# Mixer front: time-step projection and softplus one chunk earlier, the running sum and its exponentials in the third chunk, and the exponential table turned back after each part

## What is computed

```python
zxbcdt = u @ W_in.T
z0 = zxbcdt[..., :D_INNER]
x0 = zxbcdt[..., D_INNER:2 * D_INNER]
xBC = zxbcdt[..., 3 * D_INNER:3 * D_INNER + D_XBC]
dt = jax.nn.softplus(zxbcdt[..., -NHEADS:] + dt_bias)
A = -jnp.exp(A_log)
xBC = silu(causal_depthwise_conv(xBC, conv_w) + conv_b)      # 4 taps
x, Bm, Cm = split(xBC)                                       # 256, 16, 16 wide
def step(h, inp):
    x_t, B_t, C_t, dt_t = inp
    dA = jnp.exp(dt_t * A)[:, :, None, None]
    h = dA * h + dt_t[:, :, None, None] * x_t[..., None] * B_t[:, None, None, :]
    y_t = jnp.einsum('bhpn,bn->bhp', h, C_t) + D_param[None, :, None] * x_t
    return (h, y_t)
y = layernorm(scan(step)) * ln_gamma + ln_beta
y = sigmoid(y @ W_gate.T + b_gate) * y
return jnp.concatenate([_silu(z0) * x0, y], axis=-1) @ W_out.T
```

## Time and profile before

| | us |
|---|---|
| median of 3 runs | 1300.09 (1297.62 to 1300.29) |
| the profiled execution | 1297.34 |
| its span, first to last instruction | 1295.6 |
| mean granted TensorE clock | 0.967 |
| PE busy (matmul) | 1148.4 (89%) |
| DVE busy | 875.9 (68%) |
| ACT busy | 746.5 (58%) |
| POOL busy | 284.4 (22%) |

### The profile page before, as it was taken

One profiled execution on the slowest core, in us unless ns is written; L12 is line 12 of the kernel. 1 busy time (PEld: TensorE's weight loads), 2 busy tenths in 40 slices (PEclk: granted clock), 3 DMA queues, 4 the chain that ended last, 5 costly groups with the idle time before them and its releaser, 6 DMA issues.

```text
span 1295.6 us, 15745 instructions
## 1 busy us (share of the span) xinstructions
PE 1148.4 (89%) x5715; PEld 586.4 (45%) x5776; DVE 875.9 (68%) x1660; ACT 746.5 (58%) x1116; POOL 284.4 (22%) x212
## 2 busy tenths in 40 slices
PE   5789777888999999989999999999978888779998
PEld 2455443443333333333323465655533333347776
DVE  4788658967887888888853453443369998964443
ACT  4777542455655656556688654445657676435554
POOL 4223421210000000000011100100069788830000
PEclk9789889999999999999999999999989998889999
DMA  5211553344000000000000222211123232200000
GB/s 154 85 38 51 163 122 77 90 108 96 2 2 1 2 1 1 2 1 1 1 19 18 77 69 65 82 44 35 36 106 114 83 113 95 85 1 1 9 9 17
DMA packets 30492, 67.27 MB, mean 52 GB/s; under 512 B 3816, under 2 KB 16112, under 8 KB 28368
## 3 DMA queue, kind: packets, MB, share of 16 engines
q1 hardware_dynamic: 30416, 66.27, 17.5%
HBM read 57.47 MB, written 8.78 MB: 51 GB/s over the span
## 4 chain that ended last, share of the span: by engine, by line
PE 56%; DVE 15%; issue 8%; POOL 7%; ACT 7%; DMA 1%; SPq 0%; DVEq 0%; POOLq 0%; ACTq 0%
PE psum L1606 8%; PE psum L1314 8%; DVE mx L1225 7%; PE psum L1213 7%; PE psum L1282 6%; PE psum L386 5%; PE psum L388 5%; PE psum L387 5%; POOL drive L2034 5%; DVE hst L2056 2%; ACT probs L1296 2%; ACT psum L1994 1%; PE psum L454 1%; PE psum L1285 1%; PE psum L520 1%
## 5 line engine op out<-in xcount | busy, mean ns | idle before, releaser
L1225 DVE TENSOR_REDUCE mx<-psum 128x1 f32<-128x512 f32 (+3 forms) x640 | 350.4, 605 | 69.3 <-PE psum L1213 33.2
L1296 ACT ACTIVATE probs<-psum 128x1024 f32<-128x1024 f32 (+1 forms) x320 | 283.7, 937 | 178.1 <-PE psum L1282 95.0
L1213 PE MATMUL psum<-kz,qa 128*128 128x512 bf16 (+3 forms) x601 | 188.2, 352 | 24.3 <-DVE mx L1225 16.9
L1282 PE MATMUL psum<-qa,kz 128*128 128x512 bf16 (+1 forms) x618 | 175.6, 360 | 8.6 <-DMA qa<-m_rows 3.9
L1314 PE MATMUL psum<-probs,v 128*32 128x512 f32 (+3 forms) x1280 | 150.7, 542 | 1.1
L1624 DVE TENSOR_TENSOR hid<-hid,gate_bc 128x1024 f32<-128x1024 f32 x64 | 79.0, 1242 | 106.7 <-ACT hid L1616 105.0
L2034 POOL TENSOR_TENSOR drive<-du,b_bc 128x1024 f32<-128x1024 f32 x64 | 148.7, 2355 | 1.5 <-issue 1.5
L1985 PE MATMUL psum<-hst,ident 128*128 128x512 f32 x256 | 121.6, 620 | 21.9 <-DVE u L2074 14.1
L1213 PEld LDWEIGHTS psum<-kz,qa 128*128 128x128 bf16 x640 | 56.9, 97 | 182.1 <-DVE mx L1225 132.0
L1616 ACT ACTIVATE hid<-psum,cols 128x512 f32<-128x512 f32 x128 | 84.7, 689 | 75.4 <-PE psum L388 75.1
L2056 DVE TENSOR_TENSOR_SCAN hst<-psum,hlast,drive 128x512 f32<-128x512 f32 x96 | 115.0, 1262 | 8.2 <-ACT psum L1994 6.4
(11 more groups left out here) (284 smaller groups left out, 1747.9 us busy)
## 6 DMA issues: line engine op xcount, KB each, us to landing
b_bc<-b_rows SPq DMA_DIRECT2D x16, 1024.0 KB, 4.7
cs_bc<-cs_rows SPq DMA_DIRECT2D x16, 512.0 KB, 4.8
gate_bc<-gate_rows SPq DMA_DIRECT2D x32, 256.0 KB, 3.2
qk_part_rows<-qk_parts SPq DMA_DIRECT2D x48, 128.0 KB, 2.3
ew_raw<-experts_dram SPq DMA_DIRECT2D x8, 512.0 KB, 3.7
qa<-qk_part_rows SPq DMA_DIRECT2D x16, 192.0 KB, 5.3
kz<-qk_part_rows SPq DMA_DIRECT2D x16, 192.0 KB, 5.9
fw_raw<-net_dram SPq DMA_DIRECT2D x11, 256.0 KB, 2.8
```

Of the source, the lines that this page charges most:

```text
L1213: ins = pe.matmul(out[:, 0:w], qa[:, b, h // 2, i * P:(i + 1) * P], key_rows(h, c)[:, 0:w], start=True, stop=not last, skip_group_check=True)
L1225: dve.tensor_reduce(mx[:, 4 * i + h % 4, c:c + 1], fill_bank("mx", k, n)[:, 0:w], AX.X, ALU.max).then_inc(S["mx_read"], 1)
L1282: ins = pe.matmul(out[:, lo:], key_rows(h, kt // TPB)[:, kt % TPB * P:(kt % TPB + 1) * P], qa[:, b, h // 2, lo:], start=True, stop=not dia ...
L1296: act.activation(probs[:, st % 2, hh, :, lo:], s_pair[n % 2][:, :, lo:], ACT.Exp, scale=SCALE).then_inc(S["p_done"], 1)
```

## The change

The time-step projection moves from part 2 to part 1 on PE and its softplus from part 2 to part 1 on ACT. `dtA` and the running sum move from part 3 to part 2 on DVE, ahead of taps 0 and 1. On ACT the exponentials `ecs` and `eb` move from part 3 to part 2 and stand ahead of the SiLUs for `sz`. Tap 2 moves to the late half of part 2, behind `skip`; tap 3 stays in part 3. After parts 1, 2 and 3 ACT does one exponential of one column into a tile of its own, `table_ahead`, whose value nobody reads; it brings the exponential's table back there. A block then has six table loads instead of five (24 in the mixer instead of 20). The order of the ring is the same, but PE takes DTREP one chunk earlier.

```diff
--- before.py
+++ after.py
@@ -224,6 +224,7 @@
             bufs.append(sb(f"{n}_odd", [P, BLK], F32))
         qk_f = sb("qk_f", [P, 2, BLK], F32)
         qk_r = sb("qk_r", [P, 2, BLK], F32)
+        table_ahead = sb("table_ahead", [P, 3 * NB], F32)
         assert BASE + free[0] <= nc.sbuf_usable_end
 
 
@@ -415,8 +416,8 @@
         TURN_Y = [2] * (NB - 1) + [1]
 
         def mixer_fills(what, b, n):
-            return {("front", 0): [("x", b, 0)], ("front", 1): [("pj", b, j) for j in PJ_ORDER[0:2]],
-                    ("front", 2): [("pj", b, j) for j in PJ_ORDER[2:7]], ("front", 3): [("pj", b, j) for j in PJ_ORDER[7:9]],
+            return {("front", 0): [("x", b, 0)], ("front", 1): [("pj", b, j) for j in PJ_ORDER[0:3]],
+                    ("front", 2): [("pj", b, j) for j in PJ_ORDER[3:7]], ("front", 3): [("pj", b, j) for j in PJ_ORDER[7:9]],
                     ("end", 0): [("yt", b, 0), ("yt", b, 1)], ("end", TURN_Y[b]): [("yb", b, 0), ("yb", b, 1)],
                     ("end", 3): [("gate", b, 0), ("gate", b, 1)], ("end", 4): [("out", b, 0)],
                     ("end", 5): [("mix", b, 0)], ("prep", 1): [("px", b, 0)],
@@ -442,7 +443,7 @@
                 pe.wait_ge(S["xT_hi"], b + 1)
                 if b == 0:
                     pe.wait_ge(S["in_win"], 16)
-                for j in PJ_ORDER[0:2] if part == 1 else PJ_ORDER[2:7]:
+                for j in PJ_ORDER[0:3] if part == 1 else PJ_ORDER[3:7]:
                     out = ring.take(pe, "pj", b, j)
                     pe.matmul(out[:, :], w_raw[:, j * P:(j + 1) * P], x0T[:, CONV - 1:], start=True, stop=True).then_inc(S["pj_filled"], 1)
             if part == 3:
@@ -556,16 +557,11 @@
                 act.wait_ge(S["conv_hist"], b + 1)
                 for j in (BREP, CREP):
                     act.activation(convin[:, j - BREP, CONV - 1:], pj(j), ACT.Copy).then_inc(S["pj_act"], 1)
-            elif part == 2:
                 if b >= 2:
                     act.wait_ge(S["dt_done"], b - 1)
                     act.wait_ge(S["turned"], 2 * TPB * (b - 1))
                 act.activation(dt[b % 2][:, :], pj(DTREP), ACT.Softplus, bias=C("dt_bias")).then_inc(S["pj_act"], 1)
-                if b >= 1:
-                    act.wait_ge(S["pj_dve"], 2 * b)
-                for n, j in enumerate((Z0A, Z0B)):
-                    act.activation(sz[:, n, :], pj(j), ACT.Silu).then_inc(S["pj_act"], 1)
-            elif part == 3:
+            elif part == 2:
                 if b >= 2:
                     act.wait_ge(S["state_done"], TPB * (b - 1) + 1)
                 act.wait_ge(S["cs_done"], b + 1)
@@ -576,11 +572,19 @@
                     cc = slice(c * P, (c + 1) * P)
                     ins = act.activation(eb[:, cc], cs[b % 2][:, cc], ACT.Exp, scale=-1.0, bias=cs[b % 2][:, (c + 1) * P - 1:(c + 1) * P])
                 ins.then_inc(S["eb_done"], 1)
+                if b >= 1:
+                    act.wait_ge(S["pj_dve"], 2 * b)
+                for n, j in enumerate((Z0A, Z0B)):
+                    act.activation(sz[:, n, :], pj(j), ACT.Silu).then_inc(S["pj_act"], 1)
+            elif part == 3:
                 for n, j in enumerate((BREP, CREP)):
                     act.wait_ge(S["conv_done"], 2 * b + n + 1)
                     act.activation(xs[b % 2][:, j, :], cacc[:, n, :], ACT.Silu, bias=C("conv0_b", j)).then_inc(S["xs_ready"], 1)
                 for j in (XA, XB):
                     act.activation(xs[b % 2][:, j, :], pj(j), ACT.Silu, bias=C("conv0_b", j)).then_inc(S["xs_ready"], 1)
+            if part in (1, 2, 3):
+                at = 3 * b + part - 1
+                act.activation(table_ahead[:, at:at + 1], one[:, 0:1], ACT.Exp)
 
         cs_rows = nc.dram_tensor("cs_rows", (NB, TPB, H0, P), F32, kind="Internal").ap()
         cs_in = [sem(f"cs_in{n}") for n in range(CS_SLOTS)]
@@ -678,12 +682,6 @@
                 ln_stats_dve(o, dve, b, src)
                 ln_apply_dve(dve, b, src, xn, 0)
             elif part == 2:
-                dve.wait_ge(S["conv_hist"], b + 1)
-                if b >= 1:
-                    dve.wait_ge(S["xs_ready"], 4 * b)
-                conv0_dve(o, dve, b, (0, 1))
-            elif part == 3:
-
                 dve.wait_ge(S["pj_act"], 5 * b + 3)
                 dve.tensor_scalar(dtA[:, :], dt[b % 2][:, :], a_neg[:, 0:1], None, ALU.mult).then_inc(S["dt_done"], 1)
                 dve.wait_ge(S["dt_done"], b + 1)
@@ -694,7 +692,13 @@
                     ins = dve.tensor_tensor_scan(cs[b % 2][:, cc], one[:, 0:1].broadcast_to([P, P]), dtA[:, cc], 0.0,
                                                  ALU.mult, ALU.add)
                 ins.then_inc(S["cs_done"], 1)
-                conv0_dve(o, dve, b, (2, 3))
+                dve.wait_ge(S["conv_hist"], b + 1)
+                if b >= 1:
+                    dve.wait_ge(S["xs_ready"], 4 * b)
+                conv0_dve(o, dve, b, (0, 1))
+            elif part == 3:
+
+                conv0_dve(o, dve, b, (3,))
 
         def front_late_dve(o, dve, b, part):
 
@@ -711,6 +715,7 @@
                     dve.wait_ge(S["pj_filled"], 9 * b + PJ_ORDER.index(X0A) + n + 1)
                     dve.wait_ge(S["pj_act"], 5 * b + 4 + n)
                     dve.tensor_tensor(skip[:, b % 3, n, :], ring.bank("pj", b, X0A + n)[:, :], sz[:, n, :], ALU.mult).then_inc(S["pj_dve"], 1)
+                conv0_dve(o, dve, b, (2,))
 
 
         def front_pool(o, pool, b, part):
```

## The result

The changed kernel takes **1308.78 us** (median; 1306.17 to 1314.85), the kernel before, on the same chip, 1299.03 (1297.62 to 1300.29). The ratio is 1.0091, 95% interval 1.0069 to 1.0114: slower by 9 to 15 us. The forecast was 1300.8 with a range to 1304.5; the result lies above it, and above the slower rival's 1303.9.

A forecast was written before the change was run, and what follows sets the result against it. PE was taken to set the pace between 80 and 137 us, with no engine full before. Terms -0.8 + 1.4 - 2.1 + 0.25 + 1.95 = +0.7 us on the median 1300.09 gave 1300.8, range 1294.5 to 1304.5.

The forecast's parts named there:

- Rival 1: Slower: low clock stays before chunk 4, up to 1 us more in block 3; +3.8, 1303.9 us; chance 0.26.
- the far end of a term: Block 3's worst case, +3.4 us, if the clock falls after PE's new 2.7 us pause and the slow stretch isn't covered.
- Block 0, -0.8: Start of the mixer: table load leaves the path before `edec` of chunk 0, partly lost behind it; ends -1.8 and 0.
- Block 1, +1.4: Chunks 1 to 3: running sum early, but later steps on ACT and DVE give it back; ends +1.0 and +2.2.
- The chain of 20.8 us: Block 1, copy of C to the end of `cdec`: steps in the new order sum to 20.8 us, before 19.4.
- the sentence on the slack: Block 1: a clock fall after PE's new wait at chunk 3, about 2.5 us, lies ahead of XA and XB, with slack.
- Between block 1 and block 2, -2.1: Behind chunk 4's start: PE's 3.08 us pause shrinks to 0 to 2, full clock returns; ends -3.4 and +0.
- Block 2, +0.25: Chunks 5 and 6: `sz`, which PE waits for next, comes at 88.3 instead of 88.05; ends 0 and +0.6.
- One sign: Block 2: PE's wait for `mdec` of chunk 5, which ended at 79.65, would end over a microsecond sooner.
- Block 3, +1.95: Third projection waits about 2.7 us for the bank that `yn` frees; yb 1 near 125.9, not 123.95; ends +1.5, +3.4.
- Attention and behind: After the mixer: no instruction moves, and attention waits for the last block's output, so the sum carries to the end.
- Rival 2: Faster: table loads leave the path before chunks 0, 4, 8, 12, 4 x 1.3 = 5.2 us; 1294.9 us; chance 0.22.

The follow-up runs named there:

- e1: Changed kernel plus two idle matmuls in each of PE's four new pauses, no wait shortened: 1300.29 us, ratio 1.0029 to the kernel before.
- f4: Changed kernel plus two idle matmuls at one place only, the wait for `sz` ahead of the second yb of block 0: 1304.74 us, ratio 1.0057.
- e4: Kernel before with only the exponential's table turned back ahead, by one-column exponentials after parts 2 and 3: 1297.21 us, ratio 0.9997.
- f1: Kernel before plus idle matmuls in two of its own pauses, three ahead of chunk 4 and two ahead of px 0: 1295.06 us, ratio 0.9986.
- h1: Kernel before with the table turned back ahead and idle matmuls in four pauses: ahead of chunk 4, px 0, v of block 0, px 1: 1296.18 us, ratio 0.9993.
- e3: Changed kernel with the two SiLUs of `sz` put ahead of the exponentials in part 2: 1302.59 us, ratio 1.0051.
- g1: Changed kernel with `sz` ahead of the exponentials in every block and block 3's time-step projection and softplus back in part 2: 1306.71 us, ratio 1.0062.

## Why the prediction was wrong

The step that failed is the treatment of PE's new waits. The sum priced the chains that end in these waits and put the clock behind them at nothing: in block 1 because the slow stretch "lies ahead of XA and XB, which have slack", in block 2 without asking, in block 3 as the far end of a term. The runs show 7 to 8 us there, of the 9.8 that the medians moved: e1 keeps PE busy in the four waits and has them back. The rest is the path, 3.4 us from chunk 3 on in e1, where the terms of blocks 1 to 3 add up to +1.5. By its steps, starts from the profiled executions:

- **Block 0, -0.8.** Right in kind, small: `edec` of chunk 0 from 32.48 to 32.12, -0.36. The running sum took twice its time beside POOL's work, as the far end said, and block 0 has a wait of PE for `sz` that it did not have. ACT's, DVE's and PE's timelines:

```profile
32.12 2.44 ACT L619 ACTIVATE edec<-cs_bc,ncs_tok 128x128 f32<-128x128 f32 x8 [0.88 <-DVE ncs_tok L745]
```

```profile
17.29 2.76 DVE L692 TENSOR_TENSOR_SCAN cs_even<-one,dtA 128x128 f32<-128x128 f32 x4
```

```profile
23.84 3.70 PE L455 MATMUL psum<-x0T,wk 128*128 128x512 f32 x8 [1.37 <-ACT sz L578]
```

- **Block 1, +1.4: the first step that failed.** The chain of 20.8 us was sized well: `cdec` ended at 67.19, forecast 66.7. What failed is the sentence on the slack. It was PE's old pause of 3.08 us. The new pause took 2.43 of it and the low clock another 3.1 (from the `xs` transposes to the end of XB PE now needed 12.4 us, before 9.3), so PE itself was last: chunk 4 started at 68.55, +2.43. From chunk 3 to chunk 4 the kernel before took 12.72 us, the changed one 15.33 and e1, with that pause filled, 13.94: the path cost 1.2, about as forecast, and the clock 1.4 more. The pause itself came as the prediction had it, by DVE: from `dtA`, which waits for the softplus, to `mdec` it never stands still, and `mdec` starts at 54.80, before at 52.32. `edec` of chunk 2 is late too (50.54, before 47.34), but POOL's masks of it end at 54.01, ahead of that. ACT's and DVE's timelines:

```profile
47.13 1.28 ACT L563 ACT_TABLE_LOAD   x1
48.43 0.69 ACT L563 ACTIVATE dt_odd<-psum,cols 128x512 f32<-128x512 f32 x1
```

```profile
49.15 0.49 DVE L686 TENSOR_SCALAR dtA<-dt_odd,a_neg 128x512 f32<-128x512 f32 x1 [0.39 <-ACT dt_odd L563]
...
51.73 1.78 DVE L670 SCALAR_TENSOR_TENSOR cacc<-convin,cols,cacc 128x512 f32<-128x512 f32 x2
...
54.80 1.28 DVE L757 TENSOR_TENSOR mdec<-edec,psum 128x512 f32<-128x512 f32 x2
```

- **Between block 1 and block 2, -2.1.** Right: the clock was full behind chunk 4 (1.00 from 68.5 to 75.6), and the lag behind the kernel before fell from 2.43 to 0.52 us at chunk 5, -1.9.
- **Block 2, +0.25.** The copy of C came 1.05 us late and yb 1 1.44, so the step up to yb 1 cost 0.4. But the sum stopped at the wait. I had not asked what a wait for `sz` of 2.27 instead of 1.17 us does to the clock behind it, on the stretch that I had myself named as PE's. It cost 3.36 us, and f4 gives back 3.1 of them alone. One sign failed as well: the wait for `mdec` of chunk 5 should have ended over a microsecond sooner than 79.65; it ended at 80.85.
- **Block 3, +1.95.** The ring's wait came as drawn (2.73 us, ended by `yn`, ahead of the third projection). Behind it yb 1 was 4.2 us later than the +4.80 carried in, not 1.95: my chain left out the softplus's own table load (1.28), and the third projection ran at 1.2 GHz, so ACT's load began 2.17 us behind its start instead of 1.14. ACT's timeline:

```profile
123.44 1.28 ACT L563 ACT_TABLE_LOAD   x1 [4.27 <-PE psum L448]
124.74 0.69 ACT L563 ACTIVATE dt_odd<-psum,cols 128x512 f32<-128x512 f32 x1
...
126.84 2.43 ACT L619 ACTIVATE edec<-cs_bc,ncs_tok 128x128 f32<-128x128 f32 x8
129.18 0.61 ACT L570 ACTIVATE ecs_odd<-cs_odd 128x512 f32<-128x512 f32 x1
...
130.98 1.28 ACT L578 ACT_TABLE_LOAD   x1
132.28 1.09 ACT L578 ACTIVATE sz<-psum 128x512 f32<-128x512 f32 x2
```

  The wait of 2.53 us brought one more low stretch (0.76), and the gates stood at +10.60. In e1 the way from chunk 8 to chunk 12 still takes 3.6 us more than before, so most of this block's loss is path: here the size of the term was wrong as well.
- **Attention and behind.** It carries the sum, as said. In this one execution 7 us more come on up to the end, at lower clocks in places that have no changed instruction (0.94 against 0.98 from 215 to 300 us); that is about what the execution has over the median.
- **Rivals.** Rival 1 named the right cause at the wrong place and two fifths of the size: it let the low clock stay behind chunk 4, where it went, and allowed 1 us for a new fall where two stretched PE's work by over 3 us each: +3.8 where the medians show +9.8. Rival 2 fell with the result, and e4 shows its table loads to be worth nothing by themselves. Of the rule on a drain with each switch of tables: the softplus of 48.43 starts 0.02 us after its load's end here too. The prediction's "near +3" for it should read 3.5 (0.7 and twice 1.38). The trace disagrees with the rule (the Trainium skill, ScalarE: Activation LUTs, What ACT_TABLE_LOAD costs).

With its four new pauses filled (e1) the change costs 0.29%, 3.8 us, inside the range but 3 us above the forecast. The clock's part, 8 us, I had priced as a rival with a quarter of the chance.

## What to carry to other kernels

On a stretch that PE bounds, price a new or longer wait of PE with what follows it: read the granted clock behind the waits of that size that the trace has, and where they are low, count the stretch at half speed as part of the wait. When an instruction moves ahead on one engine, list what now stands behind it there (`edec`, `sz`) as carefully as what it brings sooner. Where a wait can't be removed, a few idle matmuls into a free bank can be worth more than the reordering. A higher clock is not yet a gain, though: f1 and h1 raised it in two stretches each and gained less than expected or nothing.

## What the runs showed of the hardware

The length of a pause alone did not settle what the clock did. The wait of 2.36 us for `mdec` of chunk 2 in e3 and in g1, and that of 1.72 and 1.73 for `mdec` of chunk 6 inside the front of chunk 7, were followed by opposite clocks in the two kernels (e3's windows, then g1's):

```profile
52.20:59.20 7.00, 6.96 (x33) 4.19 (x34) 6.89 (x23) 6.70 (x17) 2.56 (x3) 0.76 0.29 105
85.00:92.00 7.00, 6.97 (x37) 3.89 (x38) 6.90 (x23) 6.54 (x16) 2.56 (x3) 1.00 0.23 90
```

```profile
53.40:60.40 7.00, 7.00 (x37) 3.87 (x38) 6.90 (x23) 6.70 (x17) 2.56 (x3) 1.00 0.30 118
85.20:92.20 7.00, 6.96 (x33) 4.17 (x34) 6.90 (x23) 6.54 (x17) 2.56 (x3) 0.76 0.21 81
126.50:133.50 7.00, 6.82 (x30) 4.12 (x31) 6.90 (x25) 3.11 (x10) 2.55 (x3) 0.50 0.24 95
```

So a wait of that size is a risk rather than a fixed price. The executions of e3 went from 1297.95 to 1306.33; that such falls make the spread is likely but not shown, since only one of them has a trace. What else decides was not tried. And four `tensor_tensor_scan` of 128x128 took 2.76 us in block 0, where POOL was masking the tile `blank` (`affine_select`, two of 128x512), and 1.37 in the kernel before in block 0 and in both kernels in block 1; that POOL is the reason was not tested.
